# Causal mask of a fused attention kernel: from a TensorE accumulation to an operand of the VectorE copy out of PSUM

## What is computed

```python
k = jnp.einsum('ihd,bpd->biph', W_K, x)
q = jnp.einsum('ihd,bpd->biph', W_Q, x)
v = jnp.einsum('ihd,bpd->biph', W_V, x)
scores = jnp.einsum('biph,biqh->biqp', k, q)
mask = jnp.tril(jnp.ones((pos, pos), dtype=x.dtype))
masked = scores * mask - jnp.float32(10000000000.0) * (1.0 - mask)
attn = jax.nn.softmax(masked / jnp.sqrt(jnp.float32(d_head)), axis=-1)
z = jnp.einsum('biqp,biph->biqh', attn, v)
```

## Time and profile before

| what | value |
|---|---|
| median of three runs | 2338.56 us (2337.83 to 2340.6) |
| the profiled execution | 2341.84 us, its span 2339.8 us |
| TensorE matmul, weight load | busy 2235.7 us (96%), 1909.9 us (82%) |
| VectorE, ScalarE, GpSimd | busy 1218.2 us (52%), 975.6 us (42%), 632.7 us (27%) |
| mean granted TensorE clock | 0.982 |

### The profile page before, as it was taken

The page is one execution under the profiler, slowest core; times in us unless marked ns, Lnnn a source line. Parts: engine busy times, 40 slices in busy tenths (PEclk is TensorE's granted clock), DMA queues, the critical chain, the costliest instruction groups (busy, mean ns, idle before and its releaser), DMA issues. The chain is left out here.

```text
span 2339.8 us, 38212 instructions
## 1 busy us (share of the span) xinstructions
PE 2235.7 (96%) x12912; PEld 1909.9 (82%) x12912; DVE 1218.2 (52%) x2846; ACT 975.6 (42%) x1852; POOL 632.7 (27%) x470
## 2 busy tenths in 40 slices
PE   5899999999999999999999999999958888999899
PEld 3788888888888888888888888888847676888787
DVE  7364655656565565656555464555635553111465
ACT  4354544545455454545545454555523322111211
POOL 3435262543526254352601011010333330000000
PEclk8999999999999999999999999999979999999999
DMA  5111111101111110111100000000157763000121
GB/s 193 39 46 35 35 34 41 51 23 45 34 34 34 43 49 23 45 34 34 34 30 24 14 20 11 25 9 26 37 177 227 215 215 108 18 27 27 37 67 63
DMA packets 102320, 133.32 MB, mean 57 GB/s; under 512 B 9984, under 2 KB 68224, under 8 KB 102272
## 3 DMA queue, kind: packets, MB, share of 16 engines
q1 hardware_dynamic: 84128, 120.62, 16.2%
q10 hardware_dynamic: 18144, 12.06, 1.6%
HBM read 90.83 MB, written 33.95 MB: 53 GB/s over the span
## 5 line engine op out<-in xcount | busy, mean ns | idle before, releaser
L963 DVE TENSOR_SCALAR_CACHE_REDUCE probs<-ps_s 128x512 f32<-128x512 f32 (+3 forms) x640 | 371.2, 607 | 263.2 <-PE ps_t L830 116.8
L974 DVE TENSOR_TENSOR pT_lo<-ps_t,pT_hi 128x512 fp32r<-128x512 f32 (+3 forms) x640 | 368.6, 605 | 242.8 <-ACT pT_hi L895 241.6
L895 ACT ACTIVATE pT_hi<-ps_t 128x512 fp32r<-128x512 f32 (+3 forms) x640 | 318.7, 531 | 230.4 <-PE ps_t L830 229.6
L906 ACT ACTIVATE probs<-probs,rmin 128x128 f32<-128x128 f32 (+15 forms) x256 | 308.1, 1203 | 150.1 <-DVE rmin L967 124.9
L190 PE MATMUL ps_z<-pT_hi,v_hi 128*128 128x256 f32 (+1 forms) x1152 | 333.7, 290 | 0.3 <-issue 0.3
L190 PE MATMUL ps_p<-hT_hi,w_hi 128*128 128x512 f32 x768 | 320.7, 418 | 8.3 <-POOL halves L708 3.7
L191 PE MATMUL ps_z<-pT_lo,v_hi 128*128 128x256 f32 (+1 forms) x1152 | 324.8, 282 | 0.0
L192 PE MATMUL ps_z<-pT_hi,v_lo 128*128 128x256 f32 (+1 forms) x1152 | 324.7, 282 | 0.0
L830 PE MATMUL ps_t<-ident,probs 128*128 128x128 f32 x2176 | 309.6, 273 | 8.3 <-ACT probs L906 5.8
L192 PE MATMUL ps_p<-hT_hi,w_lo 128*128 128x512 f32 x768 | 303.5, 395 | 0.0
L191 PE MATMUL ps_p<-hT_lo,w_hi 128*128 128x512 f32 x768 | 301.6, 393 | 0.0
(11 more groups left out here) (146 smaller groups left out, 3685.7 us busy)
## 6 DMA issues: line engine op xcount, KB each, us to landing
scratch_zT<-z SPq DMA_DIRECT2D x256, 64.0 KB, 1.6
o_z<-scratch_zT SPq DMA_DIRECT2D x32, 512.0 KB, 4.6
o_scales<-scratch_recips SPq DMA_DIRECT2D x32, 512.0 KB, 5.7
w_raw<-in_w_qkv SPq DMA_DIRECT2D x16, 768.0 KB, 4.7
p_wmod<-in_w_mod SPq DMA_DIRECT2D x6, 1024.0 KB, 10.9
words<-in_gu_packed SPq DMA_DIRECT2D x44, 128.0 KB, 3.4
scratch_wgu<-deq_a SPq DMA_DIRECT2D x22, 256.0 KB, 2.0
g_wraw<-scratch_wgu SPq DMA_DIRECT2D x11, 512.0 KB, 3.5
```

What stands on the lines that cost most here:

```text
L895: nc.scalar.activation(pT[0][:, slot, i % 2, 0:w], ps_t[:, (chunks_before(i) + u) % 2, 0:w], ACT.Copy).then_inc(t_hi, 1)
L906: nc.scalar.activation(probs[:, i % 2, 0:w], probs[:, i % 2, 0:w], ACT.Exp, bias=rmin[:, i % 2:i % 2 + 1], scale=-1.0, accum_out=sums[:, i ...
L963: nc.vector.tensor_scalar(probs[:, i % 2, c * BT:c * BT + w], ps_s[:, at % NB, 0:w], 1.0, None, ALU.mult, ALU.min, accum_out=least).then_i ...
L974: nc.vector.tensor_tensor(pT[1][:, slot, i % 2, 0:w], ps_t[:, (chunks_before(i) + u) % 2, 0:w], pT[0][:, slot, i % 2, 0:w].bitcast(F32), A ...
```

## The change

The tile `causal` becomes 512 columns wide and fp32: 384 columns of zeros and behind them the triangle, so that its last w columns are the mask of a diagonal chunk of width w. TensorE's fourth matmul is gone, and `scores_ready` is on the third. [...] The copies of other chunks stay as they were.

```diff
-                    causal=sb("causal", [P, P], BF16, both), zeros=sb("zeros", [P, P], F32, both),
+                    causal=sb("causal", [P, BT], F32, both), zeros=sb("zeros", [P, P], F32, both),
...
-        pool.wait_ge(start.consts, 1)
-        nc.gpsimd.affine_select(out=start.causal[:, :], in_=start.zeros[:, :], compare_op=ALU.is_ge, fill=MASKED,
+        nc.gpsimd.memset(start.causal[:, 0:BT - P], 0.0).then_inc(start.consts, 1)
+        pool.wait_ge(start.consts, 2)
+        nc.gpsimd.affine_select(out=start.causal[:, BT - P:BT], in_=start.zeros[:, :], compare_op=ALU.is_ge, fill=MASKED,
...
-            diagonal = c == b
-            last = split_matmul(nc, ps_s[:, at % NB, 0:n], q, k, True, True)
-            if diagonal:
-                last = nc.tensor.matmul(ps_s[:, at % NB, r * P:(r + 1) * P], ident_bf[:, :], causal[:, :],
-                                        start=False, stop=True, skip_group_check=True)
-            last.then_inc(scores_ready, 1)
+            split_matmul(nc, ps_s[:, at % NB, 0:n], q, k, True, True).then_inc(scores_ready, 1)
...
-            nc.vector.tensor_scalar(probs[:, i % 2, c * BT:c * BT + w], ps_s[:, at % NB, 0:w], 1.0, None,
-                                    ALU.mult, ALU.min, accum_out=least).then_inc(row_copied, 1)
+            out = probs[:, i % 2, c * BT:c * BT + w]
+            if c < nch - 1:
+                ins = nc.vector.tensor_scalar(out, ps_s[:, at % NB, 0:w], 1.0, None, ALU.mult, ALU.min, accum_out=least)
+            else:
+                nc.vector.memset(lead[:, i % 2:i % 2 + 1], 0.0)
+                ins = nc.vector.tensor_tensor_reduce(out=out, in0=ps_s[:, at % NB, 0:w], in1=causal[:, BT - w:BT],
+                                                     scale=1.0, scalar=3e38, op0=ALU.add, op1=ALU.min,
+                                                     accum_out=least)
+            ins.then_inc(row_copied, 1)
```

More of the change, by code:

```diff
@@ L553, in attention @@
     z = sb("z", [P, ZBUF, 2 * P], F32)
+    lead = sb("lead", [P, 2], F32)
     cmin = sb("cmin", [P, 2, NB], F32)
@@ L708, in _ @@
         nc.gpsimd.memset(halves[:, :], 0.5).then_inc(consts, 1)
-        pool.wait_ge(consts, 3)
+        pool.wait_ge(consts, 4)
         def split_weights(h, m, n):
@@ L863, in head @@
                 run(h + op.shift, op)
-        pe.wait_ge(consts, 2)
         for op in shifted(PE_OPS, 1):
@@ L1001, in head @@
                     run(h + op.shift, op)
+        dve.wait_ge(consts, 3)
         for op in shifted(DVE_OPS, 1):
```

## The result

The changed kernel takes 2317.85 us (median of five runs, 2313.48 to 2324.86) against 2338.56 us before; the ratio is 0.9907, with a 95% interval of 0.9884 to 0.9929. That is 20.7 us less; 18.4 us were forecast, and the range held it. The profiled execution took 2318.8 us, 23.0 less than that of before. In a later comparison the ratio was 0.9882 (0.9864 to 0.9900), 26.9 us between the medians.

The account below looks back on a forecast made before the run. It took TensorE to bound the kernel, with waits at `T6.0` in heads that unpack weights. Savings of 9.1 + 1.2 + 8.1 = 18.4 us from the median of 2338.56 gave 2320.2 us, range 2310 to 2329.

Parts of the forecast that it names:

- What bounds the kernel: Whole kernel: TensorE's weight loads waited for exponentials 11 times, 8.0 us in all, in the heads that unpack weights.
- The price of a mask: TensorE, diagonal chunks: 0.12 us ahead of wider matmuls, 0.07 ahead of transposes; 1.62 us a head, 25.9 in all.
- Where it is given back: `S2.0` to `T6.0`, heads 0 to 10: 0.62 us saved on six masks becomes a longer wait at `T6.0`.
- The edits on the chain: `S2.0` to `T6.0`, heads with unpacking: scores 0.07 us earlier, two `memset`s at 0.08 us each; net -0.09 us saved.
- The custom instruction: VectorE, replacing the copy with a minimum: its second operand is free, 0 us added, about 0.69 us for 512 columns.
- The sum: All heads: 9.1 us in heads 1 to 10, 1.2 in head 0, 8.1 in heads 11 to 15; 18.4 us.
- all is saved: Rival, all heads: the chain gets quicker or starts earlier, so the whole 25.9 us come, 2312.7 us; chance 0.10.
- a mask is worth its columns only: Rival, TensorE: 0.05 us for each mask's 128 columns, 8.5 us saved in all, 2330.1 us; chance 0.06.
- The slow copy: Rival, VectorE: custom copy slower by the column, up to 9.9 us lost; between 2324 and 2330.1 us, chance 0.09.
- the large fixed cost: Rival, custom instruction twice per head between `S2.0` and `T6.0`: about 2345 us at 1.0 us each; chance 0.06.
- What the profile would show: Profile after: `T6.0` waits some 0.7 us longer in heads 1 to 10, about 7 us; `S2.0` to `X1` within 0.1.
- new waits at splits: Sign in the profile after: new waits at `UQ1` or at splits would mean the 18.4 us total is wrong.

Follow-up runs that it names:

- masks_in: The changed kernel with TensorE's mask matmul back in the six diagonal chunks of row blocks 2 to 7, between `S2.0` and `T6.0`: 2320.26 us, ratio 0.9921.
- masks_all: The changed kernel with TensorE's mask matmul back in all 16 diagonal chunks of a head, beside the new copy: 2339.31 us, ratio 1.0002.
- memset5: The changed kernel with five memsets on different columns ahead of each custom copy instead of one: 2319.51 us, ratio 0.9912.

## Why the prediction was right, point by point

- *What bounds the kernel* held: TensorE, apart from the waits in each head with unpacking. In the earlier trace rows it is busy for 1608.79 of 1617.00 us at a granted clock of 1.00, VectorE for 909.13. What TensorE no longer issued was won where nothing else made it wait: 1.85 us in each of heads 11 to 14.
- *The price of a mask* was too low: 1.62 us forecast for a head, 1.85 measured. One cause is a miscount. "In the list of TensorE's steps 6 of a head's 16 diagonal chunks are followed by transposes" is wrong: `S15.3` is followed by a projection, so it is 5 and 11, which gives 1.67. The rest is size: the ten masks outside the stretch cost 1.19 us, the six inside 0.64 (forecast 1.00 and 0.62). Place by place, in head 12 of the profiles before and after, a mask ahead of a wider matmul cost 0.11 to 0.18 us, 0.136 on average, and not always the 0.12 of the one place in the earlier trace rows; ahead of transposes it was 0.05 to 0.09, on average the 0.07 forecast.
- *Where it is given back* held in place and size: 0.62 us forecast, and masks_in shows 0.64 - 0.05 = 0.59 us lost there.
- *The edits on the chain* were forecast at 0.09 us more and measured (102.24 - 100.90) - 1.19 = 0.15 us less. The 0.07 us at its head came as said. The two `memset`s and custom copies cost 0.02 us at most in masks_all, not 0.16: I took a small instruction's duration for its cost, and it lies beside the next one. The other 0.1 us lies in the transfer, on which nothing was changed: it took 3.33 us on average from the request of the words to `X1` in the profile before, 3.23 after, and 3.27 in the repeat of the changed kernel. I take it for scatter.
- *The custom instruction* costs what the copy before did, as said:

```profile
L964 DVE CUSTOM_DVE_ANT_0 probs<-ps_s,causal 128x512 f32<-128x512 f32 x64 | 43.9, 686 | 0.0
L964 DVE CUSTOM_DVE_ANT_0 probs<-ps_s,causal 128x128 f32<-128x128 f32 x64 | 18.3, 286 | 78.4 <-issue 78.4
L963 DVE MEMSET lead<- 128x1 f32 x256 | 15.1, 59 | 1.1 <-PE ps_s L192 1.0
```

It is 686 ns against 687 in the earlier trace rows for 512 columns, and 286 against 287 for 128; before:

```profile
L963 DVE TENSOR_SCALAR_CACHE_REDUCE probs<-ps_s 128x128 f32<-128x128 f32 x64 | 18.4, 287 | 80.7 <-PE ps_s L819 80.7
```

So it has neither a larger fixed cost nor a larger one by the column.

- *The sum:* heads 1 to 10 gave 13.4 us (forecast 9.1), head 0 1.1 (1.2), heads 11 to 15 the other 9.1 (8.1). The miscount, the price of a mask and the term of the chain err the same way, so 18.4 us became 23.6 between the score matmuls. That the medians of the first comparison lay only 20.7 us apart, nearer to the forecast, is partly luck: in the later one they lay 26.9 apart.
- *The rivals.* That all is saved would have shown 1.85 us in every head. That a mask is worth its columns only falls with 1.85 instead of 0.80 us in a head. The 1.85 us are 0.116 us for each mask. The slow copy and the large fixed cost fall with the rows above.
- *What the profile would show:* the waits. I had put the 0.7 us of growth in each head, 7 us in all, at `T6.0` alone. The row of the waits that answers to the earlier trace rows went from 8.0 to 9.6 us only, since `Z2.0` waits first; its row stood at 0.8 us, 2 times, before:

```profile
PEld ps_t L827 <- ACT probs L902: 9.6, 12, 2.3
PEld ps_z L190 <- issue: 6.7, 10, 0.9
```

In head 7 the distance ahead of `Z2.0` grew by 0.48 us, that behind its first matmul by 0.08 and that ahead of `T6.0` by 0.15, together 0.71. The forecast named new waits at splits as a sign that its sum is wrong. This is one, since `Z2.0` waits for a split; but it lies in the same stretch and gives back the same saving, so it moved the place and left the sum. From `S2.0` to `X1` head 7 had 19.52 us in both profiles; the average over heads 1 to 10 fell from 19.64 to 19.47 us, a little more than the 0.1 us allowed.

## What to carry to other kernels

On a full TensorE (busy for 1609 of 1617 us) a matmul of 128 columns cost more here than its columns: 0.11 to 0.18 us ahead of wider ones, where its columns alone would be some 0.05, an estimate from the 0.23 us of 512. So price it from starts in the trace, with and without it. Moving its work into an operand of a copy that ran anyway cost nothing here (masks_all). Before counting such a gain, ask for each stretch whether something that holds no TensorE work (here GpSimd, a queue and a transfer, tied in at two places of a written order) sets its end: of what was saved in there, 0.59 of 0.64 us in a head were lost here. The cure can be a single word: `X1` behind `L6.1` gave 11.7 us more between medians and 12.6 between the score matmuls, about half of the 23.6 us that the change gave there.

## What was not expected of the hardware

- In memset5 `memset`s of one column follow each other at 9 ns though each shows 59 ns, and the custom copy behind them is shown from 790.96 us, 0.01 us behind the first of them (790.95): four more cost 0.04 us together.
- The 0.07 us by which a mask's end lay behind the third matmul's came through unchanged over 15 us of work on VectorE, GpSimd and SyncE's queue: `X0` 0.93 to 0.86 us, the request of the words 16.31 to 16.25 us after `S2.0` on average.
- The transfer at the end of that chain took from 3.20 us (masks_in) to 3.37 us (memset5) on average over heads 1 to 10, though no edit touches it, and since `T6.0` hangs on it this goes into the time of ten heads. Of one kernel there are only two profiles, 3.23 and 3.27 us. With `X1` moved, heads 1 to 14 of an execution agree to within 0.04 us.
